# A relational graph layer with residual and normalisation: the low parts of x go from GpSimd to VectorE, the variance step the other way, and the order of three engines' programs is changed

## The chip, the core and the metric

One core of one Trainium2 chip. The kernel is one program on that core, with five instruction streams written out by hand: TensorE (PE), VectorE (DVE), ScalarE (ACT), GpSimd (POOL), and SyncE (SP), which only issues DMAs. They meet through semaphores. The metric is the device time of one execution in microseconds, median of several; lower is better.

## What is computed

The inputs are x (8 batches, 1024 rows, 128 features, fp32), adj (8 x 1024 x 1024, int32, mostly 0 and 1), four weights of 128 x 128 and a bias. Cut to what matters:

```python
rel_ids = arange(1, 5)
masks = (adj[None] == rel_ids[:, None, None, None])        # r b n m
h = einsum('rbnm,bmd->rbnd', masks, x)
y = einsum('rbnd,rdo->bno', h, weight) + bias
t = x + y
out = (t - mean(t)) / sqrt(var(t) + 1e-5)                   # over the 128 features
```

The fast path computes relation 1 alone, and on the way it finds out whether adj holds any value above 1. Only if it does, a second, general path behind a branch computes all again; with these inputs it is not entered.

## The kernel before, in words

**Tiling.** A batch of adj (4 MB) comes in 4 *units* of 1 MB, so there are 32 units, u = 0 to 31, two of them to a *half* (hf = 0 to 15), two halves to a batch (b = 0 to 7). Unit u is 2048 int32 to each of 128 partitions. Eight units fit in `adj_sb` (NADJ, L30), four batches of x (0.5 MB each) in `x_sb`.

**The way of a unit.** SP loads it. DVE converts it to bytes (`convert`, L425, the instruction is L429, tile `mask`, four buffers). PE *turns* it: four transposes into PSUM (`turn`, L558; L178, tile `tp_ps`, three buffers). ACT *expands* the turned bytes to fp32r (`expand`, L346; L350, tile `maskT`, four buffers). When both units of a half are expanded, PE multiplies them with x: 8 matmuls with the high part of x (`hi_products`, L577), 8 with the low part (`lo_products`, L586), all at L187. ACT copies the result to SBUF (`copy_half`, L353, L357), and PE projects it with the weight (`project_half`, L564: one matmul that spreads the bias, L194, and 8 at L199, tile `y_ps`, two buffers).

**The end of a half.** DVE adds x (`add_half`, L443, tile `total`), takes the statistics (`measure_half`: four at L205, four at L210), and adds epsilon to the variance (`lift_variance`, L214, tile `var_eps`). POOL (`scales`, L302) makes minus the mean (L307), the reciprocal root by a power (L217, tile `scale`), and their product (L312, tile `shift`). The four row tiles of the half are then normalised, two by DVE (`finish_half`, L221), one half later, and two by ACT (`finish_half`, L370), later still. SP stores whole batches once all loads are issued.

**The split of x.** For the products x is split into two fp32r parts. Before: DVE masks off bits to get `x_top` (`top`, L432, instruction L166, one buffer), POOL copies that to `x_hi` (`hi`, L293, L297), and POOL subtracts it from x to get `x_lo` (`lo`, L299, L170). Both parts have two buffers by batch. `x_top` of a batch waits until POOL has finished both parts of the batch before it.

**The order of the work.** Each engine executes its stream in order, and the order is that of the loops:

- SP (L239): unit 0, x of batch 0, then the units; x of batch 1 behind unit 3, of batch 2 behind unit 6, of batch b+1 behind unit 4b+2. A unit's load from u = 8 on waits for the conversion of unit u-8, x of batch b from b = 4 on for the last add of batch b-4.
- PE (L607): warm-up, the first half in quarters, and from hf = 2 (L628): hi products of hf, turn of unit 2hf+3, projection of half hf-1, lo products of hf, turn of unit 2hf+4.
- ACT (L387): copy of half hf-1, expansion of units 2hf+2 and 2hf+3, finish of half hf-3.
- DVE (L495 to L512): convert 0, top 0, the bias, converts 1 to 3, top 1, converts 4 and 5; then for hf = 1 to 14: converts 2hf+4 and 2hf+5, for even hf the top of batch hf/2+1, add and measure of half hf-1, finish of half hf-2.
- POOL (L318 to L331): split of the bias, hi and lo of batch 0, then for each b: hi of b+1, scales of half 2b-1, lo of b+1, scales of half 2b.

`place_bias` (L488) copies the three bf16 parts of the bias, each repeated four times, into `bias_parts`; its three copies (L491) stand ahead of convert 1.

## Time and profile before

| what | value |
|---|---|
| median of 3 runs | 118.46 us (117.81 to 120.78) |
| the profiled execution, its own time | 118.53 us |
| its span in the profile | 116.7 us |
| PE busy | 102.6 us (88%) |
| DVE busy | 95.0 us (81%) |
| ACT busy | 84.6 us (72%) |
| POOL busy | 75.7 us (65%) |
| DMA, mean over the span | 361 GB/s, about 420 GB/s until all is loaded |
| granted clock of TensorE, mean | 0.991 of full speed |

The span runs from the first to the last instruction that the profile records; 1.83 us of the execution's own time lie outside it. Busy shares are means over a head that fills the pipe, a long middle in which the same half is repeated, and a tail. Weight loads run beside matmuls and are listed as an engine of their own (PEld). The ends of matmuls are modelled, so a group of 8 that is shown as 2.1 us may be followed by the next group after 1.87 us.

### The profile page before, as it was taken

The numbers are of one execution on the slowest core, as the hardware profiler recorded it, in microseconds if no ns is written. First come the engines' busy times: TensorE is split into PE (matmuls) and PEld (weight loads), VectorE is DVE, ScalarE is ACT, GpSimd is POOL, SyncE is SP. The second block draws the span as 40 slices with busy tenths as digits, with TensorE's granted clock in tenths as the row PEclk, the third lists the DMA queues.
The fourth block names the chain that finished last, engine by engine and source line by source line (L and its number), as shares of the span: only waits on it lengthen the run. The fifth ranks groups of instructions, "written<-read, shape, count | busy, mean of one in ns | idle before, by whom it ended". The sixth has DMA issues, their size and how long they took to land.

```text
span 116.7 us, 1943 instructions
## 1 busy us (share of the span) xinstructions
PE 102.6 (88%) x587; PEld 85.5 (73%) x587; DVE 95.0 (81%) x242; ACT 84.6 (72%) x114; POOL 75.7 (65%) x78
## 2 busy tenths in 40 slices
PE   5966379994999999999999999999999999999800
PEld 2333378683889888888898889898888888889600
DVE  0089967633989899999999999999999999996960
ACT  0433199179868997899999999999999889974410
POOL 6069038000095998599759898999899759953640
PEclk9999999999999999999999999999999999999996
DMA  3999999999999999999999999999999997030441
GB/s 87 396 433 429 415 438 427 415 432 418 418 424 424 424 424 417 417 424 424 414 431 421 414 428 413 429 413 427 421 427 418 404 420 314 10 142 38 171 152 53
DMA packets 7362, 42.16 MB, mean 361 GB/s; under 512 B 819, under 2 KB 1206, under 8 KB 3254
## 3 DMA queue, kind: packets, MB, share of 16 engines
q1 hardware_dynamic: 7200, 41.95, 86.9%
q8 instruction: 6, 0.10, 0.4%
q10 hardware_dynamic: 150, 0.07, 0.2%
q14 instruction: 6, 0.05, 0.1%
HBM read 37.82 MB, written 4.19 MB: 360 GB/s over the span
## 4 chain that ended last, share of the span: by engine, by line
PE 48%; DMA 21%; DVE 15%; POOL 8%; issue 3%; ACTq 1%; POOLq 0%; DVEq 0%
PE h_ps L187 32%; DMA adj_sb<-in_adj_dram 17%; PE y_ps L199 8%; PE tp_ps L178 7%; DMA bias_rows<-in_L_gnn_bias_dram 4%; DVE bias_parts L491 4%; POOL scale L217 4%; DVE mask L429 3%; DVE stats L205 3%; POOL x_lo L170 2%; DVE total L443 2%; PE y_ps L194 2%; DVE var_eps L214 2%; DVE mean_var L210 1%; ACTq L379 1%
## 5 line engine op out<-in xcount | busy, mean ns | idle before, releaser
L350 ACT ACTIVATE maskT<-tp_ps 128x2048 fp32r<-128x2048 fp8e5 x32 | 60.2, 1881 | 14.9 <-PE tp_ps L178 14.8
L429 DVE TENSOR_SCALAR mask<-adj_sb 128x2048 uint8<-128x2048 uint32 x32 | 39.5, 1267 | 12.4 <-DMA adj_sb<-in_adj_dram 12.4
L217 POOL TENSOR_TENSOR scale<-var_eps,power 128x4 f32<-128x4 f32 (+1 forms) x17 | 36.3, 2137 | 0.9 <-DVE var_eps L214 0.7
L187 PE MATMUL h_ps<-maskT,x_hi 128*128 128x512 f32 (+1 forms) x144 | 34.2, 379 | 2.6 <-ACT maskT L350 2.5
L187 PE MATMUL h_ps<-maskT,x_lo 128*128 128x512 f32 (+1 forms) x144 | 34.3, 380 | 0.4 <-POOL x_lo L170 0.4
L187 PEld LDWEIGHTS h_ps<-maskT,x_hi 128*128 128x128 f32 x144 | 24.3, 189 | 7.7 <-ACT maskT L350 3.9
L187 PEld LDWEIGHTS h_ps<-maskT,x_lo 128*128 128x128 f32 x144 | 24.1, 189 | 4.5 <-POOL x_lo L170 0.7
L178 PEld LDWEIGHTS tp_ps<-identity,mask 128*128 128x128 f32 x128 | 19.8, 202 | 6.4 <-DVE mask L429 2.7
L178 PE MATMUL tp_ps<-identity,mask 128*128 128x128 f32 x128 | 20.2, 281 | 3.4 <-DVE mask L429 3.4
L170 POOL TENSOR_TENSOR x_lo<-x_sb,x_top 128x1024 fp32r<-128x1024 f32 x8 | 19.2, 2402 | 0.0
L307 POOL TENSOR_SCALAR minus_mean<-mean_var 128x4 f32<-128x4 f32 (+1 forms) x16 | 4.0, 248 | 22.5 <-DVE var_eps L214 21.6
L199 PEld LDWEIGHTS y_ps<-w_sb,h_sb 128*128 128x128 f32 x128 | 16.7, 192 | 1.2 <-ACT h_sb L364 0.7
L199 PE MATMUL y_ps<-w_sb,h_sb 128*128 128x128 f32 x128 | 17.2, 276 | 0.3 <-ACT h_sb L364 0.3
L205 DVE BATCH_NORM_STATS2 stats<-total 128x6 f32<-128x128 f32 x64 | 14.1, 281 | 1.3
L370 ACT ACTIVATE out_sb<-total,shift,scale 128x128 f32<-128x128 f32 x31 | 13.5, 484 | 0.8 <-POOL shift L312 0.6
L297 POOL CAST x_hi<-x_top 128x1024 fp32r<-128x1024 f32 x8 | 8.3, 1041 | 6.9 <-DVE x_top L166 6.9
L357 ACT ACTIVATE h_sb<-h_ps 128x512 f32<-128x512 f32 x14 | 8.4, 599 | 5.5 <-issue 5.5
L443 DVE TENSOR_TENSOR total<-y_ps,x_sb 128x512 f32<-128x512 f32 (+1 forms) x17 | 11.0, 650 | 0.8 <-PE y_ps L199 0.8
L221 DVE TENSOR_SCALAR out_sb<-total,mean_var,scale 128x128 f32<-128x128 f32 x33 | 9.9, 339 | 0.6 <-POOL scale L217 0.6
L214 DVE TENSOR_SCALAR var_eps<-mean_var 128x4 f32<-128x4 f32 (+1 forms) x17 | 8.3, 485 | 1.7
L605 PE MATMUL h_ps<-warm 128*128 128x512 bf16 x24 | 7.6, 478 | 1.4 <-POOL warm L275 1.4
L312 POOL TENSOR_TENSOR shift<-minus_mean,scale 128x4 f32<-128x4 f32 (+1 forms) x16 | 6.0, 372 | 2.1
(30 smaller groups left out, 40.4 us busy)
## 6 DMA issues: line engine op xcount, KB each, us to landing
adj_sb<-in_adj_dram SPq DMA_DIRECT2D x32, 1024.0 KB, 18.0
x_sb<-in_x_dram SPq DMA_DIRECT2D x8, 512.0 KB, 12.1
out_dram<-out_sb SPq DMA_DIRECT2D x7, 512.0 KB, 18.5
out_dram<-out_sb SPq DMA_DIRECT2D x1, 256.0 KB, 2.3
out_dram<-out_sb SPq DMA_DIRECT2D x2, 128.0 KB, 2.6
w_sb<-in_L_gnn_weight_dram ACTq DMA_DIRECT2D x1, 64.0 KB, 7.1
bias_rows<-in_L_gnn_bias_dram ACTq DMA_DIRECT2D x3, 0.5 KB
```

What stands on the lines that cost most here:

```text
L170: eng.tensor_tensor(flat(x_lo[:, slot]), flat(x_sb[:, x_slot]), flat(x_top[:, :]).bitcast(fp32), ALU.subtract).then_inc(done, 1)
L178: last = nc.tensor.transpose(tp_ps[:, bank, place:place + P], words[:, o, j], identity[:, :])
L187: last = nc.tensor.matmul(h_ps[:, bank, 0:n], (x_hi, x_lo)[part][:, slot, t, :], maskT[:, places, t // WORD, t % WORD, :], start=(first an ...
L199: last = nc.tensor.matmul(y[:, n, :], h_of(r)[:, s], w_sb[:, r, :], start=False, stop=(r == relations - 1 and s == tiles.stop - 1))
L205: last = nc.vector.bn_stats(stats[:, slot, s, :], total[:, place, s, :])
L214: nc.vector.tensor_scalar(var_eps[:, slot, tiles], mean_var[:, slot, tiles, 1], EPS, None, ALU.add).then_inc(done, by)
L217: nc.gpsimd.tensor_tensor(scale[:, slot, tiles], var_eps[:, slot, tiles], power[:, tiles], ALU.pow).then_inc(done, by)
L221: last = nc.vector.tensor_scalar(out_sb[:, b, s, :], total[:, place, s, :], mean_var[:, slot, s, 0:1], scale[:, slot, s:s + 1], ALU.subtra ...
L350: nc.scalar.activation(maskT[:, u % NMT], turned_codes(u % NTP), ACT.Copy, accum_out=counts[:, u:u + 1]).then_inc(expanded, 1)
L370: last = nc.scalar.activation(out_sb[:, b, s, :], total[:, b % NTOTAL, s, :], ACT.Identity, bias=shift[:, b % 2, s:s + 1], scale=scale[:, ...
L429: nc.vector.tensor_scalar(mask[:, u % NMASK], adj_sb[:, u % NADJ].bitcast(u32), CAP, SET, ALU.min, ALU.mult).then_inc(masked, 1)
L443: nc.vector.tensor_tensor(total[:, b % NTOTAL, tiles], y, x_sb[:, b % NX, tiles], ALU.add).then_inc(added, by)
```

## The change

`x_top` is gone. POOL makes `x_hi` by a copy of x that rounds to fp32r (DVE does it for batch 0), and DVE makes `x_lo`, as x minus `x_hi`, for all batches. The step that adds epsilon to the variance goes from DVE to POOL, as the first instruction of `scales`. DVE's stream is shifted by one conversion: in iteration hf it converts units 2hf+3 and 2hf+4 (was 2hf+4 and 2hf+5); at its start the bias copies stand behind convert 2 and are a quarter as wide. PE projects half hf-1 ahead of the turn of unit 2hf+3. ACT finishes half hf-3 between its two expansions. SP loads x of batch b+1 behind unit 4b+3. The bias matmul reads one row block of the bias, repeated by its access pattern. The diff without its declarations and without the general path (which gets the same split of x):

```diff
--- before.py
+++ after.py
@@ -68,7 +66,7 @@
         bias_rows = sb("bias_rows", [P, D], fp32)
         bias_rest = sb("bias_rest", [P, D], fp32)
         bias_fine = sb("bias_fine", [P, D], fp32)
-        bias_parts = sb("bias_parts", [P, HT, D], bf16)
+        bias_parts = sb("bias_parts", [P, D], bf16)
         spread = sb("spread", [P, P], bf16)
         identity = sb("identity", [P, P], fp32)
         ones = sb("ones", [P, P], fp32)
@@ -162,12 +159,8 @@
         def store(eng, b, place, tiles, done):
             eng.dma_start(out_p[b][:, tiles.start * D:tiles.stop * D], flat(out_sb[:, place, tiles])).then_inc(done, 16)
 
-        def take_top(x_slot, done):
-            nc.vector.tensor_scalar(flat(x_top[:, :]), flat(x_sb[:, x_slot]).bitcast(u32), TOP_BITS, None,
-                                    ALU.bitwise_and).then_inc(done, 1)
-
         def take_lo(eng, x_slot, slot, done):
-            eng.tensor_tensor(flat(x_lo[:, slot]), flat(x_sb[:, x_slot]), flat(x_top[:, :]).bitcast(fp32),
+            eng.tensor_tensor(flat(x_lo[:, slot]), flat(x_sb[:, x_slot]), flat(x_hi[:, slot]).bitcast(fp32),
                               ALU.subtract).then_inc(done, 1)
 
         def turn_words(of, bank, done):
@@ -191,7 +184,8 @@
 
         def spread_bias(y, tiles):
             n = tiles.stop - tiles.start
-            nc.tensor.matmul(y[:, 0:n, :], spread[:, :], bias_parts[:, 0:n, :], start=True, stop=False)
+            nc.tensor.matmul(y[:, 0:n, :], spread[:, :], bias_parts[:, :].unsqueeze(1).to_broadcast([P, n, D]),
+                             start=True, stop=False)
 
         def project(h_of, y, relations, tiles, done, by):
             for n, s in enumerate(range(tiles.start, tiles.stop)):
@@ -210,8 +204,8 @@
                 last = nc.vector.bn_aggr(mean_var[:, slot, s, :], stats[:, slot, s, :])
             last.then_inc(done, by)
 
-        def lift_variance(slot, tiles, done, by):
-            nc.vector.tensor_scalar(var_eps[:, slot, tiles], mean_var[:, slot, tiles, 1], EPS, None, ALU.add).then_inc(done, by)
+        def lift_variance(eng, slot, tiles, done, by):
+            eng.tensor_scalar(var_eps[:, slot, tiles], mean_var[:, slot, tiles, 1], EPS, None, ALU.add).then_inc(done, by)
 
         def row_scales(slot, tiles, done, by):
             nc.gpsimd.tensor_tensor(scale[:, slot, tiles], var_eps[:, slot, tiles], power[:, tiles], ALU.pow).then_inc(done, by)
@@ -240,7 +234,7 @@
             load_batch(0)
             for u in range(1, UNITS):
                 load_unit(u)
-                if u % CH == (2 if u >= CH else 3) and u // CH + 1 < B:
+                if u % CH == CH - 1 and u // CH + 1 < B:
                     load_batch(u // CH + 1)
             for b in range(LAST):
                 sp.wait_ge(normed, CH * (b + 1))
@@ -280,7 +274,7 @@
                                     channel_multiplier=1).then_inc(const_set, 1)
             nc.gpsimd.memset(power[:, :], -0.5).then_inc(const_set, 1)
             nc.gpsimd.memset(spread[:, :], 1.0).then_inc(const_set, 1)
-            nc.gpsimd.memset(bias_parts[:, :, :], 0.0).then_inc(bias_split, 1)
+            nc.gpsimd.memset(bias_parts[:, :], 0.0).then_inc(bias_split, 1)
 
             def split_bias():
                 pool.wait_ge(bias_loaded, 16 * len(PARTS))
@@ -291,21 +285,22 @@
                                         ALU.subtract).then_inc(bias_split, 1)
 
             def hi(b):
-                pool.wait_ge(topped, b + 1)
-                if b >= 2:
+                pool.wait_ge(x_loaded[b % NX], 16 * (b // NX + 1))
+                if b == 1:
+                    pool.wait_ge(lo_made, 1)
+                else:
                     pool.wait_ge(multiplied, CH * (b - 1))
-                nc.gpsimd.tensor_copy(flat(x_hi[:, b % 2]), flat(x_top[:, :]).bitcast(fp32)).then_inc(hi_made, 1)
-
-            def lo(b):
-                take_lo(nc.gpsimd, b % NX, b % 2, lo_made)
+                nc.gpsimd.tensor_copy(flat(x_hi[:, b % 2]), flat(x_sb[:, b % NX])).then_inc(hi_made, 1)
 
             def scales(b, tiles, count, by):
-                pool.wait_ge(var_ready, count)
+                pool.wait_ge(aggregated, count)
                 if b >= 2:
                     pool.wait_ge(normed, CH * (b - 1))
                     pool.wait_ge(act_normed, CH * (b - 1))
+                lift_variance(nc.gpsimd, b % 2, tiles, var_ready, by)
                 nc.gpsimd.tensor_scalar(minus_mean[:, b % 2, tiles], mean_var[:, b % 2, tiles, 0], -1.0, 0.0,
                                         ALU.mult, ALU.add).then_inc(negated, by)
+                pool.wait_ge(var_ready, count)
                 row_scales(b % 2, tiles, scaled, by)
                 pool.wait_ge(scaled, count)
                 pool.wait_ge(negated, count)
@@ -316,17 +311,15 @@
                 scales(hf // 2, HALF[hf % 2], 2 * (hf + 1), 2)
 
             split_bias()
-            hi(0)
-            lo(0)
             for b in range(B):
                 if b + 1 < B:
                     hi(b + 1)
                 if b >= 1:
                     scales_half(2 * b - 1)
-                if b + 1 < B:
-                    lo(b + 1)
                 scales_half(2 * b)
             scales(LAST, QUARTER[2], 2 * (HALVES - 1) + 1, 1)
+            pool.wait_ge(aggregated, 2 * HALVES)
+            lift_variance(nc.gpsimd, LAST % 2, QUARTER[3], var_ready, 1)
             pool.wait_ge(var_ready, 2 * HALVES)
             row_scales(LAST % 2, QUARTER[3], scaled, 1)
@@ -384,13 +376,14 @@
             expand(2)
             copy_quarter(0, 1)
             expand(3)
-            for hf in range(1, HALVES - 1):
-                if hf >= 2:
-                    copy_half(hf - 1)
+            expand(4)
+            expand(5)
+            for hf in range(2, HALVES - 1):
+                copy_half(hf - 1)
                 expand(2 * hf + 2)
-                expand(2 * hf + 3)
                 if hf >= 3:
                     finish_half(hf - 3)
+                expand(2 * hf + 3)
             copy_half(HALVES - 2)
             finish_half(HALVES - 4)
             copy_quarter(HALVES - 1, 0)
@@ -429,12 +422,9 @@
                 nc.vector.tensor_scalar(mask[:, u % NMASK], adj_sb[:, u % NADJ].bitcast(u32), CAP, SET,
                                         ALU.min, ALU.mult).then_inc(masked, 1)
 
-            def top(b):
-                dve.wait_ge(x_loaded[b % NX], 16 * (b // NX + 1))
-                if b >= 1:
-                    dve.wait_ge(hi_made, b)
-                    dve.wait_ge(lo_made, b)
-                take_top(b % NX, topped)
+            def lo(b):
+                dve.wait_ge(hi_made, b + 1)
+                take_lo(nc.vector, b % NX, b % 2, lo_made)
 
             def add(b, y, tiles, count, by):
                 dve.wait_ge(projected, count)
@@ -449,8 +439,6 @@
             def variances(b, tiles, count, by):
                 dve.wait_ge(measured, count)
                 aggregate_rows(b % 2, tiles, aggregated, by)
-                dve.wait_ge(aggregated, count)
-                lift_variance(b % 2, tiles, var_ready, by)
 
             def finish(b, tiles, count, by):
                 dve.wait_ge(scaled, count)
@@ -488,24 +476,25 @@
             def place_bias():
                 dve.wait_ge(bias_split, 3)
                 for q, part in zip(PARTS, (bias_rows, bias_rest, bias_fine)):
-                    last = nc.vector.tensor_copy(bias_parts[q:q + 1], upper(part[q:q + 1, :]).unsqueeze(1).to_broadcast(
-                        [1, HT, D]))
+                    last = nc.vector.tensor_copy(bias_parts[q:q + 1, :], upper(part[q:q + 1, :]))
                 last.then_inc(bias_split, 1)
 
             convert(0)
-            top(0)
+            dve.wait_ge(x_loaded[0], 16)
+            nc.vector.tensor_copy(flat(x_hi[:, 0]), flat(x_sb[:, 0])).then_inc(hi_made, 1)
+            lo(0)
+            convert(1)
+            convert(2)
             place_bias()
-            for u in (1, 2, 3):
-                convert(u)
-            top(1)
+            convert(3)
             convert(4)
-            convert(5)
+            lo(1)
             for hf in range(1, HALVES - 1):
-                for u in (2 * hf + 4, 2 * hf + 5):
+                for u in (2 * hf + 3, 2 * hf + 4):
                     if u < UNITS:
                         convert(u)
                 if hf % 2 == 0 and hf // 2 + 1 < B:
-                    top(hf // 2 + 1)
+                    lo(hf // 2 + 1)
                 add_half(hf - 1)
                 measure_half(hf - 1)
                 if hf >= 2:
@@ -627,9 +616,8 @@
             turn(6)
             for hf in range(2, HALVES - 1):
                 hi_products(hf)
-                if 2 * hf + 3 < UNITS:
-                    turn(2 * hf + 3)
                 project_half(hf - 1)
+                turn(2 * hf + 3)
                 lo_products(hf)
                 if 2 * hf + 4 < UNITS:
                     turn(2 * hf + 4)
```

## Rows read from the trace of the kernel before

**Rows 1.** The page's first line: span and instructions of the profiled execution.

```profile
span 116.7 us, 1943 instructions
```

**Rows 2.** Windows view, all engines: stretch and its length, then busy us (instructions), clock.

```profile
51.20:74.20 23.00, 23.00 (x133) 20.11 (x132) 22.02 (x60) 20.75 (x28) 19.76 (x17) 1.00 1.01 421
```

**Rows 3.** The chain that ended last: start us, us, engine, tile, line.

```profile
72.56 1.86 PE h_ps L187 x8
74.41 0.46 PE tp_ps L178 x4
...
77.20 0.22 PE y_ps L194
77.41 0.89 PE y_ps L199 x8
...
101.68 3.08 PE h_ps L187 x16
```

**Rows 4.** Timeline of the head: start us, us, engine, line, operation, tiles, count.

```profile
9.27 2.49 DVE L491 COPY bias_parts<-bias_rest 1x512 bf16<-1x512 bf16 x1
...
28.02 2.13 PE L187 MATMUL h_ps<-maskT,x_hi 128*128 128x512 f32 x8 [1.58 <-ACT maskT L350]
...
31.66 1.23 DVE L429 TENSOR_SCALAR mask<-adj_sb 128x2048 uint8<-128x2048 uint32 x1
```

**Rows 5.** DMA view, issues between 6.5 and 8 us: count, KB, us to landing.

```profile
adj_sb<-in_adj_dram SPq DMA_DIRECT2D x1, 1024.0 KB, 23.9
```

**Rows 6.** Timeline of VectorE (DVE) over one batch, 80.4 to 92.4 us.

```profile
80.42 0.68 DVE L166 TENSOR_SCALAR x_top<-x_sb 128x1024 uint32<-128x1024 uint32 x1
81.02 0.68 DVE L443 TENSOR_TENSOR total<-y_ps,x_sb 128x512 f32<-128x512 f32 x1
81.80 0.87 DVE L205 BATCH_NORM_STATS2 stats<-total 128x6 f32<-128x128 f32 x4
...
82.71 0.38 DVE L210 BATCH_NORM_AGGREGATE mean_var<-stats 128x2 f32<-128x6 f32 x4
...
83.19 0.17 DVE L214 TENSOR_SCALAR var_eps<-mean_var 128x4 f32<-128x4 f32 x1
83.27 0.60 DVE L221 TENSOR_SCALAR out_sb<-total,mean_var,scale 128x128 f32<-128x128 f32 x2
...
83.78 2.36 DVE L429 TENSOR_SCALAR mask<-adj_sb 128x2048 uint8<-128x2048 uint32 x2
...
86.05 0.68 DVE L443 TENSOR_TENSOR total<-y_ps,x_sb 128x512 f32<-128x512 f32 x1
...
88.23 1.45 DVE L214 TENSOR_SCALAR var_eps<-mean_var 128x4 f32<-128x4 f32 x1
...
92.38 0.68 DVE L166 TENSOR_SCALAR x_top<-x_sb 128x1024 uint32<-128x1024 uint32 x1
```

**Rows 7.** Timeline of GpSimd (POOL) over the same batch.

```profile
83.67 3.34 POOL L217 TENSOR_TENSOR scale<-var_eps,power 128x4 f32<-128x4 f32 x1
...
87.14 0.20 POOL L312 TENSOR_TENSOR shift<-minus_mean,scale 128x4 f32<-128x4 f32 x1
87.29 2.37 POOL L170 TENSOR_TENSOR x_lo<-x_sb,x_top 128x1024 fp32r<-128x1024 f32 x1
...
93.13 1.04 POOL L297 CAST x_hi<-x_top 128x1024 fp32r<-128x1024 f32 x1 [0.61 <-DVE x_top L166]
```

**Rows 8.** Line L217, 28 to 104 us: count, ns min/median/max, first and last start.

```profile
L217 POOL TENSOR_TENSOR scale<-var_eps,power x13: 1073/2530/3947, 32.9 to 102.0; 128x4 f32<-128x4 f32 x13
```

**Rows 9.** Groups by line and form, L443 at half width: busy us, mean ns.

```profile
L443 DVE TENSOR_TENSOR total<-y_ps,x_sb 128x256 f32<-128x256 f32 x2 | 0.8, 414 | 0.0
```

**Rows 10.** Timeline, 82 to 85 us: one turn on TensorE and its expansion on ScalarE.

```profile
82.34 0.63 PE L178 MATMUL tp_ps<-identity,mask 128*128 128x128 f32 x4
...
83.00 1.88 ACT L350 ACTIVATE maskT<-tp_ps 128x2048 fp32r<-128x2048 fp8e5 x1 [0.28 <-PE tp_ps L178]
...
84.77 0.20 ACT L350 ACTIVATION_READ_ACCUMULATOR maskT<-tp_ps 128x1 f32 x1
```

More of the change, by code:

```diff
@@ L10 @@
 FULL = 2048.5
-TOP_BITS = 0xFFFFF000
 def relational_layer(nc, x, adj, weight, bias, out):
@@ L62, in relational_layer @@
         x_sb = sb("x_sb", [P, NX, TILES, D], fp32)
-        x_top = sb("x_top", [P, TILES, D], u32)
         x_hi = sb("x_hi", [P, 2, TILES, D], fp32r)
@@ L107, in relational_layer @@
         expanded = sem("expanded")
-        topped = sem("topped")
         hi_made = sem("hi_made")
@@ L129, in relational_layer @@
         g_loaded = sem("g_loaded")
-        g_topped = sem("g_topped")
+        g_hi_made = sem("g_hi_made")
         g_split = sem("g_split")
@@ L336, in _ @@
                 with pool.Fori(0, B) as b:
-                    pool.wait_ge(g_topped, b + 1)
+                    pool.wait_ge(g_hi_made, b + 1)
                     take_lo(nc.gpsimd, 0, 0, g_split)
-                    nc.gpsimd.tensor_copy(flat(x_hi[:, 0]), flat(x_top[:, :]).bitcast(fp32)).then_inc(g_split, 1)
                     pool.wait_ge(g_var_ready, b + 1)
@@ L532, in _ @@
                     nc.vector.memset(scratch[:, 0:1], 0.0)
-                    take_top(0, g_topped)
+                    nc.vector.tensor_copy(flat(x_hi[:, 0]), flat(x_sb[:, 0])).then_inc(g_hi_made, 1)
                     for r in range(R):
@@ L550, in _ @@
                     dve.wait_ge(g_aggregated, b + 1)
-                    lift_variance(0, ALL, g_var_ready, 1)
+                    lift_variance(nc.vector, 0, ALL, g_var_ready, 1)
                     dve.wait_ge(g_scaled, b + 1)
@@ L660, in _ @@
                                 turn_words(mask[:, ch], ch % NTP, g_turned)
-                            pe.wait_ge(g_split, 2 * (b + 1))
+                            pe.wait_ge(g_split, b + 1)
                             pe.wait_ge(g_expanded, CH * R * b + CH * r + 2 * half + 2)
```

## The prediction, made before the changed kernel was run

> **What bounds the kernel now.** I read the page first (the span is 116.7 us [rows 1]; the profiled execution took 118.53 us, so 1.83 us lie outside, and it stands 0.07 us above the median of the runs), then the windows, the chain, and the timelines of the engines.
>
> In the middle TensorE is the bound: 23.00 us busy in a stretch of 23.00, at full granted clock, while VectorE is busy for 22.02, ScalarE 20.75 and GpSimd 19.76 [rows 2]. The reader is to see how close the others are: VectorE has 1 us in 23 to spare. One half costs TensorE, by the chain's steps, 1.86 for the hi products, 0.46 for a turn, 0.22 and 0.89 for bias and projection, as much again as the first two for the lo products and the second turn: 2 x 1.86 + 2 x 0.46 + 1.11 = 5.75 us, 11.5 a batch [rows 3]. This runs from the hi products of half 2 at 28.02 [rows 4] to the lo products of half 14 at 101.68 [rows 3]. Behind them come 116.7 - 101.7 = 15.0 us of tail.
>
> The loads matter in the head alone: unit 8 was issued once unit 0 was converted, at about 6.9 us, and took 23.9 to land [rows 5], so it is there at 30.8, just before its conversion at 31.66 [rows 4].
>
> **The head.** The bias copies stood ahead of convert 1; the second took 2.49 us and ended at 11.76 [rows 4]. Now converts 1 and 2 go first, behind x_hi and x_lo of batch 0 (about 0.7 and 1.2 us, sized below), beside the landing of unit 1. Products of halves 1 and 2 can come some 2 us earlier than 28.02. But hi of half 3 stands behind the turn of unit 8, and unit 8 doesn't land earlier: its conversion ends at 30.8 + 1.2 = 32.0 instead of 32.9 (31.66 + 1.23 [rows 4]). So 0.9 of the 2 us can outlive it. Then comes the new order: convert 9 is no longer next. It stands behind lo of batch 2, add, measure and finish.
>
> **VectorE over a batch.** In steps from start to start [rows 6]: top 0.60, add 0.78, statistics 0.91, aggregates 0.48, epsilon step 0.08, two normalisations 0.51, two conversions 2.27, and for the second half 2.18 from the add at 86.05 to the epsilon step at 88.23, which with what follows it takes until 92.38. In that last 4.15 there are 0.51 and 2.27 again and 1.37 for the epsilon step. Sum 11.96 us. The change removes the top (0.60), both epsilon steps (0.08 + 1.37) and the wait for the aggregates ahead of each (about 0.08 twice, since the aggregates end 0.10 before the step and 0.03 is usual): 11.96 - 2.2 = 9.75. It adds lo. The trace has no subtraction of 1024 elements from SBUF on VectorE. The add is 0.68 us for 512 [rows 6] and 0.414 for 256 [rows 9]; continued by the same slope that is 1.2 us for 1024. From below it is bounded by the top, 0.68 us for 1024 with one source [rows 6], from above by the same subtraction on GpSimd, 2.37 [rows 7]. I take 1.2, or 1.15 as a step. So 10.9 us of work a batch: less than TensorE's 11.5, if VectorE never waits.
>
> The Trainium skill (VectorE: DVE Perf Modes, Side-by-side) keeps a tensor_tensor of fp32 at one element a cycle, with about 150 cycles of start; by that page lo would be (1024 + 158) / 0.96 GHz = 1.23 us, an estimate that no row here can confirm.
>
> **The wait that the change adds.** It does wait. Lo of batch c+1 (in iteration hf = 2c) waits for x_hi of that batch, which GpSimd now makes behind scales of half 2c-2 in its own stream. VectorE aggregates that half in iteration 2c-1, and between this and lo stand only the normalisations and two conversions. Before, nothing that VectorE needed within the same iteration stood behind those scales. Count from the end A of the aggregates:
>
> - VectorE: normalisations 0.5, conversions until A + 2.9; it could start lo at A + 2.8.
> - GpSimd: it takes the epsilon step at about A + 0.15 (0.2 us, as minus the mean), and the power at A + 0.5, right with the first conversion. The power takes 1.07 at the least, 2.53 in the median and 3.95 at most [rows 8]. In rows 7 it starts at 83.67, 0.11 ahead of two conversions that end at 86.14 [rows 6], and ends at 87.01, so 0.87 behind them. In the median (2.53) it ends about 0.3 behind them, and its product is done 0.3 later. I take A + 2.9 + 0.6; bounds are A + 2.9 (product done with the conversions) and A + 2.9 + 1.2 (87.14 + 0.20 against 86.14).
> - The cast: 1.04 [rows 7], and 0.1 for the semaphore.
>
> Lo starts at A + 4.64, 1.84 late (bounds 1.2 and 2.45). VectorE then needs 10.9 + 1.84 = 12.74 us a batch (12.1 to 13.35), above TensorE's 11.5. It becomes the bound. Queued behind the waiting lo are add, statistics, and conversions 4c+5 and 4c+6: the turn of unit 4c+5 on TensorE waits for them, and what is behind it.
>
> **The sum.** Lo of batch 2 starts at 31.98 (GpSimd is in time there, since VectorE waits for unit 8 itself). Then lo 1.15, add 0.78, statistics 0.91, aggregates 0.41, normalisations 0.51, conversion 1.22: unit 9 is ready at 36.96. Five periods later, lo being waited for in iterations 4, 6, 8, 10 and 12, unit 29 is ready: 36.96 + 5 x 12.74 = 100.66. From there TensorE: turn 0.46, lo 1.86, turn 0.46, hi 1.86, projection 1.11, turn 0.46 [rows 3] and 0.05 for the start make 6.26: lo of half 14 starts at 106.92 instead of 101.68, 5.24 later. The tail holds the epsilon step of the last quarter on GpSimd instead of VectorE, one hop more: 0.15. Span 116.7 + 5.24 + 0.15 = 122.1, time 122.1 + 1.83 = 123.9 us, 4.6% more than the median.
>
> **What I cost at nothing.** GpSimd loses 2.37 us a batch and gains two epsilon steps of 0.2; it waits between scales anyway. The narrower bias copies and the repeated read of the bias: the copies now lie beside the landing of unit 3, the matmul writes the same columns. If that cover is gone, under 0.5 us once. SP: unit 4b+3 is issued ahead of x of the next batch instead of behind it and no longer waits for its add, so it lands 1.2 us earlier and x 2.5 us later; x is needed by the cast a full half later. Loads are issued eight units ahead, so a slower VectorE finds them landed. ACT's finish needs a product made over an iteration before. The projection ahead of the turn moves the turn of unit 2hf+3 by 1.11: from its start to the end of its expansion are 84.97 - 82.34 = 2.63 us [rows 10], and with lo and the second turn TensorE gives it 0.46 + 1.86 + 0.46 = 2.78. That is hidden by 0.15 us, and if it isn't, it costs up to 0.1 a half where TensorE is the bound, nothing where VectorE is.
>
> **Rivals.**
>
> - *The cast gets in between (119.9 us).* If power and product are done early (1.07 at the least [rows 8]) the cast can start before the conversions end. It then holds one of them, as x_lo held the epsilon step: 88.23 + 1.45 ends with x_lo at 89.66 [rows 6, 7]. VectorE loses 1.04 instead of 1.84, a period of 11.94: 5 x 0.8 = 4.0 us less than forecast. Against it: the power starts no earlier against the conversions than before, and only its shortest durations allow it. The Trainium skill (GPSIMD Engine Reference, Specifications) says that GpSimd shares its SBUF interfaces with VectorE, with contention when VectorE uses two ports or reads two SBUF inputs. The page doesn't say who wins; rows 7 show the power losing to conversions, rows 6 the epsilon step losing to x_lo.
> - *The wait costs nothing (117.8 us, not slower).* If x_hi is made by A + 3.4, the period stays under 11.5, and TensorE is the bound from the turn of unit 9 at 37.0. Then hi of half 4 is at 37.0 + 2.78 = 39.8, ten halves of 5.75 give 97.3 for half 14, its lo comes 1.86 + 1.11 + 0.46 later, at 100.7, 1.0 before the present one: 116.7 - 1.0 + 0.15 + 1.83 = 117.7 to 117.8. The point: a wait of at most 0.6 us. For it: the work itself fits (10.9). Against: the cast alone takes 1.04, behind a product that ends with the conversions at the earliest.
> - *The head's gain is kept whole (115.5 us).* As the last, and with units 8 and 9 ready when TensorE wants them: some 2.3 us less. Against it the landing of unit 8 at 30.8.
> - *The worst of both (over 127.5 us).* Period 13.35 and a lo of 2.37: 123.9 + 5 x (0.6 + 1.2) = 132.9; with the period alone 127.
>
> **Chances.** Forecast (period 12.1 to 13.35) 0.62, its own range 120.7 to 127; cast in between 0.14; no cost 0.13; head kept 0.07; worst 0.04. The range takes in the cheap wait and the long power: 119.0 to 127.5. A measurement tells about 2% from no change here. Slower by more (over 120.8): the forecast, the worst, and a part of the second case, 0.69. Faster (below 116.1): 0.06, from the fourth case. Within: 0.25.
>
> **What would show it.** Waits of VectorE for x_hi at the subtraction, six of them, the later ones near 1.8 us; TensorE waiting for conversions at the turns of units 9, 13, 17 to 29, about 1.2 us each; its busy share in the middle near 90%; the cast starting right behind the product of an even half; lo near 1.2 us; the tail from the lo products of half 14 about 15.1 us. It is wrong if the casts end before the conversions do, or if TensorE is gapless in the middle.

## The result, and the profile after

The changed kernel took 127.29 us in the median of four runs (126.94 to 128.82), beside 118.72 for the kernel before: a ratio of 1.072, with an interval of 1.064 to 1.081. It is slower by 7%. A kernel's executions fall into a faster and a slower group, and here and below a median is over all of them, a ratio and its interval over the faster group alone. I had forecast 123.9, with 119.0 to 127.5 as the range: direction and mechanism hold, the amount was 3.4 us short. The profiled execution is the longest of the four, 128.82 us.

The page's first line, the granted clock of slice after slice, and two groups of the changed kernel:

```profile
span 127.1 us, 1928 instructions
...
PEclk9999999968999999999999999999999995999997
...
L208 POOL TENSOR_SCALAR var_eps<-mean_var 128x4 f32<-128x4 f32 (+1 forms) x17 | 30.5, 1793 | 42.0 <-DVE mean_var L204 35.2
...
L163 DVE TENSOR_TENSOR x_lo<-x_sb,x_hi 128x1024 fp32r<-128x1024 f32 x8 | 9.9, 1232 | 13.0 <-POOL x_hi L293 13.0
```

The second group is the wait that the prediction put there: VectorE stands idle for 13.0 us ahead of the subtractions. The first is one that it had not seen: adding epsilon to four numbers takes 1.79 us in the mean on GpSimd, where the kernel before had 0.17 and 1.45 for it on VectorE [rows 6].

The waits of the changed kernel, in all, times, longest:

```profile
DVE x_lo L163 <- POOL x_hi L293: 13.0, 5, 2.7
...
PE tp_ps L171 <- DVE mask L422: 12.0, 9, 2.3
```

The middle by windows, to be read beside [rows 2]: 26 us of the changed kernel.

```profile
50.00:76.00 26.00, 23.68 (x132) 19.67 (x132) 20.41 (x55) 20.51 (x28) 17.35 (x19) 1.00 1.01 422
```

TensorE, which had no gap before, now has 2.3 us of gaps in 26; VectorE, ScalarE and GpSimd have more room than they had. No engine is full. What sets the pace is a loop through two of them, and the timeline of GpSimd and VectorE over one turn of that loop shows it. It answers to [rows 6] and [rows 7]:

```profile
79.87 0.38 DVE L204 BATCH_NORM_AGGREGATE mean_var<-stats 128x2 f32<-128x6 f32 x4
80.17 0.57 DVE L215 TENSOR_SCALAR out_sb<-total,mean_var,scale 128x128 f32<-128x128 f32 x2
80.40 2.65 POOL L208 TENSOR_SCALAR var_eps<-mean_var 128x4 f32<-128x4 f32 x1 [0.51 <-DVE mean_var L204]
80.66 2.35 DVE L422 TENSOR_SCALAR mask<-adj_sb 128x2048 uint8<-128x2048 uint32 x2
83.13 0.19 POOL L301 TENSOR_SCALAR minus_mean<-mean_var 128x4 f32<-128x4 f32 x1
83.28 1.04 POOL L211 TENSOR_TENSOR scale<-var_eps,power 128x4 f32<-128x4 f32 x1
84.45 0.20 POOL L307 TENSOR_TENSOR shift<-minus_mean,scale 128x4 f32<-128x4 f32 x1
84.59 1.04 POOL L293 CAST x_hi<-x_sb 128x1024 fp32r<-128x1024 f32 x1
85.66 1.23 DVE L163 TENSOR_TENSOR x_lo<-x_sb,x_hi 128x1024 fp32r<-128x1024 f32 x1 [2.65 <-POOL x_hi L293]
86.80 0.68 DVE L433 TENSOR_TENSOR total<-y_ps,x_sb 128x512 f32<-128x512 f32 x1
```

The reader is to see the order. The aggregates end at 80.25. The epsilon step starts at 80.40, 0.26 ahead of the two conversions, and doesn't end until they do, at 83.0. Power and product come wholly behind that, then the cast, and then, at 85.66, the subtraction, for which VectorE has waited 2.65 us. The cast starts as the product ends, so it waits for its place in GpSimd's stream and not for a free buffer of x_hi. Add, statistics, the next two conversions and so TensorE's next turn stand behind it. In this trace the subtractions of batches 2 and 7 start at 32.64 and 99.39: 13.35 us a batch, where TensorE's own work is 11.5.

One of the five waits of this trace is 2.39 us. There the epsilon step gets through in 0.23, and the next small step, minus the mean, is held instead:

```profile
67.29 0.23 POOL L208 TENSOR_SCALAR var_eps<-mean_var 128x4 f32<-128x4 f32 x1 [0.50 <-DVE mean_var L204]
67.54 2.36 DVE L422 TENSOR_SCALAR mask<-adj_sb 128x2048 uint8<-128x2048 uint32 x2
67.59 2.36 POOL L301 TENSOR_SCALAR minus_mean<-mean_var 128x4 f32<-128x4 f32 x1
72.29 1.23 DVE L163 TENSOR_TENSOR x_lo<-x_sb,x_hi 128x1024 fp32r<-128x1024 f32 x1 [2.39 <-POOL x_hi L293]
```

Either way power and product stand wholly behind the conversions. The epsilon step was 0.25 ahead of them here, as it was where it was held.

### The profile page after: what moved, and what is told of

Its sections match the earlier page's. It is cut to its first block, busy times and chain, and to the rows that moved or that the text cites. A ratio compares the mean times of both kernels' runs of the same rounds, so it can differ in the third digit from the quotient of the medians.

```text
span 127.1 us, 1928 instructions
## 1 busy us (share of the span) xinstructions
PE 106.9 (84%) x586; PEld 86.1 (68%) x587; DVE 87.7 (69%) x226; ACT 83.9 (66%) x114; POOL 66.0 (52%) x86
## 4 chain that ended last, share of the span: by engine, by line
PE 41%; DMA 23%; DVE 20%; POOL 8%; issue 4%; POOLq 1%; ACT 0%; DVEq 0%
PE h_ps L180 26%; DMA adj_sb<-in_adj_dram 23%; DVE mask L422 9%; PE tp_ps L171 7%; PE y_ps L193 6%; POOL var_eps L208 4%; DVE stats L199 4%; DVE total L433 3%; DVE out_sb L215 2%; POOL scale L211 2%; PE y_ps L187 2%; POOL x_hi L293 2%; DVE mean_var L204 1%; DVE x_lo L163 1%; POOLq L327 0%
## 5 line engine op out<-in xcount | busy, mean ns | idle before, releaser
L208 POOL TENSOR_SCALAR var_eps<-mean_var 128x4 f32<-128x4 f32 (+1 forms) x17 | 30.5, 1793 | 42.0 <-DVE mean_var L204 35.2
L180 PE MATMUL h_ps<-maskT,x_hi 128*128 128x512 f32 (+1 forms) x144 | 35.5, 390 | 0.4 <-ACT maskT L342 0.3
L180 PE MATMUL h_ps<-maskT,x_lo 128*128 128x512 f32 (+1 forms) x144 | 35.7, 392 | 0.0
L171 PE MATMUL tp_ps<-identity,mask 128*128 128x128 f32 x128 | 21.9, 295 | 12.0 <-DVE mask L422 12.0
L180 PEld LDWEIGHTS h_ps<-maskT,x_lo 128*128 128x128 f32 x144 | 25.4, 198 | 4.0
L163 DVE TENSOR_TENSOR x_lo<-x_sb,x_hi 128x1024 fp32r<-128x1024 f32 x8 | 9.9, 1232 | 13.0 <-POOL x_hi L293 13.0
L211 POOL TENSOR_TENSOR scale<-var_eps,power 128x4 f32<-128x4 f32 (+1 forms) x17 | 17.0, 999 | 0.1
L293 POOL CAST x_hi<-x_sb 128x1024 fp32r<-128x1024 f32 x7 | 7.3, 1038 | 6.5 <-DMA x_sb<-in_x_dram 6.5
L204 DVE BATCH_NORM_AGGREGATE mean_var<-stats 128x2 f32<-128x6 f32 x64 | 6.2, 158 | 0.6
L187 PE MATMUL y_ps<-bias_parts,spread 128*128 128x512 bf16 (+1 forms) x17 | 6.4, 377 | 0.0
## 6 DMA issues: line engine op xcount, KB each, us to landing
x_sb<-in_x_dram SPq DMA_DIRECT2D x8, 512.0 KB, 13.1
```

What stands on the lines that cost most here:

```text
L163: eng.tensor_tensor(flat(x_lo[:, slot]), flat(x_sb[:, x_slot]), flat(x_hi[:, slot]).bitcast(fp32), ALU.subtract).then_inc(done, 1)
L171: last = nc.tensor.transpose(tp_ps[:, bank, place:place + P], words[:, o, j], identity[:, :])
L180: last = nc.tensor.matmul(h_ps[:, bank, 0:n], (x_hi, x_lo)[part][:, slot, t, :], maskT[:, places, t // WORD, t % WORD, :], start=(first an ...
L208: eng.tensor_scalar(var_eps[:, slot, tiles], mean_var[:, slot, tiles, 1], EPS, None, ALU.add).then_inc(done, by)
L211: nc.gpsimd.tensor_tensor(scale[:, slot, tiles], var_eps[:, slot, tiles], power[:, tiles], ALU.pow).then_inc(done, by)
```

## The experiments

Each is the changed kernel with one edit, if not said otherwise. Times are medians, and the ratio is to the kernel before on the same chip, whose median was 120.9 for 1 to 8, 119.5 for 9 to 11 and 119.4 for 12.

**1. The subtraction behind the finish.** VectorE's work is the same, in another order.

```diff
                 for u in (2 * hf + 3, 2 * hf + 4):
                     if u < UNITS:
                         convert(u)
-                if hf % 2 == 0 and hf // 2 + 1 < B:
-                    lo(hf // 2 + 1)
                 add_half(hf - 1)
                 measure_half(hf - 1)
                 if hf >= 2:
                     finish_half(hf - 2)
+                if hf % 2 == 0 and hf // 2 + 1 < B:
+                    lo(hf // 2 + 1)
```

> The changed kernel with one move on VectorE: the subtraction that makes x_lo of batch c+1 stands behind the finish of its iteration instead of ahead of the add. Its work is the same. Theory A (the wait for x_hi behind the scales on GpSimd sets the period): by then x_hi is nearly there (aggregates, normalisations, two conversions, add, statistics, aggregates, normalisations come to 5.4 us, the cast ends near 5.6), VectorE waits 0.3 us at most, the period falls from 13.3 to TensorE's 11.5, the time to 118 to 119 us. Theory B (VectorE's own work, or the conversions that come one later, sets the period): VectorE does the same work in the same number of instructions, the period stays above 12.5 and the time above 124 us.

118.25 us, ratio 0.979 (0.960 to 0.998). Theory A holds, B falls: the same work in the same conversions' order, and all of the loss is gone. No wait for x_hi is left in its trace.

**2. The cast ahead of the scales.** VectorE's order is untouched; GpSimd's is changed, and x_hi gets a third buffer (with the waits that its reuse needs; these lines are left out here and in 10 to 12).

```diff
             for b in range(B):
-                if b + 1 < B:
-                    hi(b + 1)
+                if b == 0:
+                    hi(1)
                 if b >= 1:
                     scales_half(2 * b - 1)
+                if b + 2 < B:
+                    hi(b + 2)
                 scales_half(2 * b)
```

> The changed kernel with VectorE's order as it is, and one move on GpSimd: the cast to x_hi of batch c+1 stands ahead of the scales of half 2c-2 instead of behind them, which takes a third buffer for x_hi. Theory A: VectorE's wait at the subtraction, 2.65 us each time, is gone (under 0.3), the period is TensorE's 11.5, the time 117.5 to 119 us. Theory B: as the work and the order of VectorE are unchanged, the period stays above 12.5 and the time above 124. If the wait is gone and the time lies between 120 and 124, conversions coming late at the turn (the second half of theory B) have a part of their own.

117.25 us, ratio 0.978 (0.965 to 0.990). The order of the queue on GpSimd made the loss. The third buffer is part of this edit, but experiment 1 removes the loss without it, and in the changed kernel the cast never waited for a buffer. With the cast moved in it, VectorE waits nowhere for x_hi, though its stream still asks for it at the same place. In the second half of the middle TensorE is gapless again:

```profile
64.00:96.00 32.00, 32.00 (x186) 26.95 (x185) 29.96 (x74) 28.09 (x40) 24.90 (x25) 1.00 1.01 419
```

**3. The epsilon step back on VectorE.**

```diff
                 aggregate_rows(b % 2, tiles, aggregated, by)
+                dve.wait_ge(aggregated, count)
+                lift_variance(nc.vector, b % 2, tiles, var_ready, by)
...
-                pool.wait_ge(aggregated, count)
+                pool.wait_ge(var_ready, count)
...
-                lift_variance(nc.gpsimd, b % 2, tiles, var_ready, by)
```

> The changed kernel with the epsilon step back on VectorE, so that GpSimd starts again with minus the mean. It tells what moving the epsilon step costs. In the trace of the changed kernel that step is held on GpSimd for 2.65 us by the two conversions and the power (1.04) and the product run wholly behind them. Theory A with this as the mis-sized term: the power starts ahead of the conversions again, the product ends 0.6 us behind them instead of 1.6, the wait falls to about 1.65 us while VectorE gains 0.35 us of work a batch: a period of 12.65 instead of 13.3, time lower by 5 x 0.65 = 3.3 us, about 124. Rival (the cast and the queue alone matter, whatever stands first in the scales): the wait stays at 2.6, the period rises to 13.6, time up by 1.5 us.

127.67 us, ratio 1.061 (1.044 to 1.077): as the changed kernel. Both expectations miss in part. Its timeline over the same place in the loop:

```profile
67.70 0.17 DVE L208 TENSOR_SCALAR var_eps<-mean_var 128x4 f32<-128x4 f32 x1
...
68.17 3.34 POOL L211 TENSOR_TENSOR scale<-var_eps,power 128x4 f32<-128x4 f32 x1
68.29 2.35 DVE L418 TENSOR_SCALAR mask<-adj_sb 128x2048 uint8<-128x2048 uint32 x2
71.64 0.20 POOL L305 TENSOR_TENSOR shift<-minus_mean,scale 128x4 f32<-128x4 f32 x1
71.78 1.04 POOL L293 CAST x_hi<-x_sb 128x1024 fp32r<-128x1024 f32 x1
72.85 1.22 DVE L163 TENSOR_TENSOR x_lo<-x_sb,x_hi 128x1024 fp32r<-128x1024 f32 x1 [2.21 <-POOL x_hi L293]
```

The wait falls from 2.65 to 2.21, not to 1.65. The power starts 0.12 ahead of the conversions and still ends 0.87 behind them, in the 3.34 form. What the wait gives back, VectorE spends again: the subtractions of batches 4 and 5 are 59.34 and 72.85, a period of 13.5. So where the epsilon step runs makes no difference to the time in this order that these few executions, on another chip than the first ones of the changed kernel, could show.

**4 and 8. Zeros multiplied while TensorE waits.** Matmuls of zeros into the PSUM bank that the turn then overwrites: 8 ahead of unit 6, 6 each ahead of units 13, 17, 21, 25 and 29. It ran twice, the second time beside the changed kernel itself (5).

```diff
-            def turn(u):
+            def turn(u, idle=0):
+                if idle:
+                    pe.wait_ge(expanded, u - NTP + 1)
+                    for _ in range(idle):
+                        nc.tensor.matmul(tp_ps[:, u % NTP], warm[:, 0:P], warm[:, :], start=True, stop=True)
                 pe.wait_ge(masked, u + 1)
...
-            turn(6)
+            turn(6, 8)
...
-                turn(2 * hf + 3)
+                turn(2 * hf + 3, 6 if hf % 2 == 1 and hf > 3 else 0)
```

> The changed kernel with matmuls on zeros while TensorE waits for a conversion: 8 ahead of the turn of unit 6, 6 ahead of the turns of units 13, 17 to 29; their results are overwritten. It tells what the clock costs. In the trace of the changed kernel the granted clock is at half from 26 to 29 us and from 104 to 107 us, in both places behind a gap of about 2 us, and 8 products take 3.4 and 3.6 us instead of 2.1. Theory C (the clock adds to the end): the clock stays at 1.00, and the time falls by the 1.5 us of the later place, 0.5 to 2 us in all, since the earlier one is partly hidden behind the landing of unit 8. Rival (the clock costs nothing that VectorE's period doesn't cover): no change within 0.3 us. The period of 13.3 stays in both.

> The same kernel as the one with zeros multiplied in the waits, now beside the changed kernel on one chip. Its trace showed the clock at 1.00 all through and 8 products of half 13 in 2.12 us. Theory C: faster than the changed kernel by 0.5 to 2 us. Rival: within 0.3 us of it, since most executions of the changed kernel do not have the second place.

> The changed kernel once more, unaltered, as the measure for the runs beside it: about 127 us, 1.06 to 1.07 of the kernel before; half clock near 27 us in its trace, with or without a second place near 105 us (theory C: with it the span is 1.5 us longer than without).

Once 127.06 us, once 125.99, the second with a ratio of 1.057 (1.051 to 1.064); the changed kernel beside it 127.69 (125.89 to 128.94). Two stretches by windows, of the changed kernel first (the last three columns are the granted clock, the share of DMA, and GB/s):

```profile
26.00:29.00 3.00, 3.00 (x10) 2.52 (x11) 2.89 (x10) 2.06 (x3) 0.98 (x1) 0.53 1.03 434
104.00:108.00 4.00, 3.72 (x12) 3.04 (x13) 3.86 (x14) 1.97 (x2) 3.29 (x5) 0.59 0.00 0
```

and of the kernel with the zeros:

```profile
26.00:29.00 3.00, 3.00 (x19) 2.44 (x19) 2.61 (x10) 2.09 (x3) 1.17 (x2) 1.00 1.03 431
104.00:108.00 4.00, 3.96 (x21) 3.44 (x22) 3.86 (x13) 3.18 (x4) 3.29 (x5) 1.00 0.00 0
```

The granted clock fell to the lower of its two levels (1.2 GHz) behind gaps of 2.3 and 1.9 us on TensorE, and with the zeros it doesn't in either trace. In the trace shown the later place costs 3.60 - 2.12 = 1.5 us, and it is on the path to the end:

```profile
104.28 0.90 PE L171 MATMUL tp_ps<-identity,mask 128*128 128x128 f32 x4 [1.89 <-DVE mask L422]
104.84 3.60 PE L180 MATMUL h_ps<-maskT,x_lo 128*128 128x512 f32 x8
```

Not every execution has it. The other trace of the changed kernel (5, span 124.8) has the same products, behind a gap of 1.86 us, at full clock:

```profile
103.98 2.10 PE L180 MATMUL h_ps<-maskT,x_lo 128*128 128x512 f32 x8
```

So the clock explains part of the scatter of the changed kernel. That the zeros make the kernel faster is not shown. The changed kernel beside them took 125.9 and 126.5, and twice 128.9 at a mean granted clock of 0.955 and 0.956; the five executions with the zeros took 125.2 to 127.0, none with a clock under 0.984. The whole 1.7 us between the medians rests on those two executions, and the first set has nothing (127.06, where the changed kernel had 127.29 on another chip). The waits and the period are as before in both.

**6. A second cast, unused.** Ahead of the real one for batches 3 to 7.

```diff
...
+                if b >= 3:
+                    nc.gpsimd.tensor_copy(flat(spare[:, :]), flat(x_sb[:, b % NX])).then_inc(spared, 1)
+                    pool.wait_ge(spared, b - 2)
                 nc.gpsimd.tensor_copy(flat(x_hi[:, b % 2]), flat(x_sb[:, b % NX])).then_inc(hi_made, 1)
```

> The changed kernel with a second, unused cast of the same size ahead of the cast to x_hi of batches 3 to 7 on GpSimd (1.04 us and 0.1 for a semaphore). Theory A: every bit of it goes into VectorE's wait, 3.7 us instead of 2.65 five times, the period rises from 13.3 to 14.4 and the time by 5 x 1.1 = 5.6 us. Theory B (VectorE's own work and order set the period): GpSimd has the room for it, no change within 1 us.

133.23 us, ratio 1.117 (1.108 to 1.126): 5.5 us more than the changed kernel beside it by the medians. The trace is of its longest execution, 135.36 us. Each of the five waits is 3.77 us, 1.12 more than 2.65. The subtractions come every 14.52 us, beside 13.35 and 13.21 in the two traces of the changed kernel, which makes 5.9 to 6.6 us over five batches. GpSimd is busy for 53% of the span, and yet 1.1 us more of it at this place costs 1.2 to 1.3 us a batch:

```profile
102.86 1.04 POOL L296 CAST spare<-x_sb 128x1024 fp32r<-128x1024 f32 x1
103.96 1.05 POOL L298 CAST x_hi<-x_sb 128x1024 fp32r<-128x1024 f32 x1
...
105.05 1.23 DVE L165 TENSOR_TENSOR x_lo<-x_sb,x_hi 128x1024 fp32r<-128x1024 f32 x1 [3.77 <-POOL x_hi L298]
```

(Lines of two timelines of that kernel, GpSimd's and VectorE's.)

**7. The conversions in the old order.**

```diff
             lo(1)
+            convert(5)
             for hf in range(1, HALVES - 1):
-                for u in (2 * hf + 3, 2 * hf + 4):
+                for u in (2 * hf + 4, 2 * hf + 5):
```

> The changed kernel with VectorE's conversions back in the order of before (units 2hf+4 and 2hf+5 in iteration hf); the wait for x_hi is as it was. Theory A: the loop of VectorE and GpSimd is the same, period 13.3 and waits 2.65; but TensorE now waits for unit 2hf+4 at the end of its iteration instead of for 2hf+3 in the middle, so the same lateness is felt a turn and 8 products (2.3 us) later: the time falls by about 2.3 us once, to 124.5 to 125.5. Theory B (the order of the conversions sets the period): the period falls below 12.5 and the time below 122.

126.53 us, ratio 1.065 (1.052 to 1.077). That is 1.2 less than the median of the changed kernel beside it, but two of that kernel's four executions took 125.9 and 126.5, and the spans of the two traces are 124.3 and 124.8. So no gain is shown, where I had expected 2.3 us. Period and waits are unchanged (the subtractions come every 13.1 us), so theory B falls here too. In the trace the 2.3 us are there but paid for beforehand: now units 8 and 9 are both converted ahead of the first subtraction of the loop, and unit 9 lands later, so the loop starts at 35.01 instead of 32.52.

**9 to 11. What is left of the rest.** 9 is the kernel before with the bias copies as in the change; 10 is the version of experiment 2 with the old order of conversions and turn; 11 is that version again.

```diff
...
             convert(0)
             top(0)
-            place_bias()
-            for u in (1, 2, 3):
-                convert(u)
+            convert(1)
+            convert(2)
+            place_bias()
+            convert(3)
             top(1)
```

> The kernel before with one part of the change alone: the copies of the bias a quarter as wide and behind convert 2. Everything else is as before, so top, cast and lo of GpSimd, the epsilon step on VectorE, conversions and projection in the old order. I expect the products of half 2 about 2 us earlier, of which the landing of unit 8 leaves 0.5 to 1: 0.4 to 0.9% faster than before, 117.5 to 118.2 us if before is 118.5. If it is over 1.5% faster, the head alone is what the version with x_hi ahead of the scales gains; if it is the same as before, the gain of that version has another source.

> The version with the cast ahead of the scales (third buffer of x_hi), and both reorderings taken back: conversions 2hf+4 and 2hf+5, the turn of unit 2hf+3 ahead of the projection. Left of the change are the split of x, the epsilon step, the bias and the head. In the trace of the version with them TensorE has no gap from half 9 on and a half costs 5.79 us, 0.03 more than before. I expect 116.3 to 117.3, up to 1 us faster than that version: 0.4 from the turn (12 x 0.03), and 0.5 from conversion 9 being early in the head. If it is slower, the reorderings were worth something with the wait gone.

> The version with the cast ahead of the scales once more, beside the two others on one chip: 1.5 to 3% faster than the kernel before.

118.12, 117.44 and 117.48 us, ratios 0.993 (0.988 to 0.997), 0.990 (0.985 to 0.995) and 0.992 (0.987 to 0.997). Experiments 2 and 11 are the same kernel: 0.978 in the first set, 0.992 in this one with more executions, where I had expected 1.5 to 3%. With the wait out of the way the whole change is worth about 1%, as much as the head alone within the measurement. The two reorderings are worth nothing either way: I had expected up to 1 us from taking them back.

**12. The best version with a warm head.** Experiment 2 with 6 matmuls of zeros ahead of unit 6 and 2 ahead of unit 8.

```diff
...
-            turn(6)
+            turn(6, 6)
...
-                    turn(2 * hf + 4)
+                    turn(2 * hf + 4, 2 if hf == 2 else 0)
```

> The version with the cast ahead of the scales (third buffer of x_hi), with matmuls on zeros in the two waits of the head: 6 ahead of the turn of unit 6, 2 ahead of that of unit 8. In the second trace of that version the granted clock is at 0.50 from 26 to 28 us, behind a gap of 2.1 us, and the hi products of half 2 take 3.4 us. Theory C: the clock stays at 1.00 there, half 3 starts up to 1.2 us earlier, the time falls by 0.3 to 1 us, to 116.3 to 117.2, or 1 to 2% under the kernel before. Rival: the landing of unit 8 covers it, the time stays at 117.4 within 0.2 us.

117.34 us, ratio 0.987 (0.981 to 0.993). The clock stays up, and nothing comes of it: the rival holds. The trace shows what covers it:

```profile
32.49 2.11 PE L181 MATMUL h_ps<-maskT,x_hi 128*128 128x512 f32 x8
...
36.47 0.74 PE L171 MATMUL tp_ps<-identity,mask 128*128 128x128 f32 x4 [0.76 <-DVE mask L425]
...
39.31 2.11 PE L181 MATMUL h_ps<-maskT,x_hi 128*128 128x512 f32 x8
```

Half 3 starts at 32.49 instead of 33.49 in experiment 11, but the turn of unit 9 then waits for its conversion, and half 4 starts at 39.31 in the one and 39.36 in the other. The kernel before had 39.58 there. Nor is the clock down there every time without the zeros: in the trace of experiment 2, the same kernel as 11, the gap ahead of unit 6 is 0.96 us, the hi products of half 2 take 2.13, and half 4 starts at 39.23.

## Why the prediction was right in kind and short in amount

**The hit.** The median of 127.29 us lies in the range of 119.0 to 127.5 by 0.2 us, above the forecast's own 120.7 to 127, and the repeat's 127.69 (5) is outside both. That the range held is in part luck.

**What bounds the kernel, and the work of VectorE.** Right. The subtraction takes 1.23 us (taken: 1.2). With no wait VectorE fits under TensorE, as experiments 1 and 2 show.

**The head.** Right in its waits, 0.5 to 0.7 us short in its sum. Unit 8 was there at about 30.7 and bounded the subtraction of batch 2, and the conversion of unit 9 came late. Half 3 starts at 33.82, as before: the hi products of half 2 ran at half clock, 3.44 us, and TensorE came to the turn of unit 8 after it had been converted. With the zeros (4) half 3 starts at 33.01. The claim that GpSimd is in time for batch 2 missed something: the cast for it ran from 30.60, and the conversion of unit 8, begun at 30.73, took 1.98 us instead of 1.23. In the versions without the wait (1, 2, 9 to 12) half 4 starts between 39.23 and 39.69, beside 39.58 before: at most 0.35 us of the head's gain reaches it.

```profile
30.60 1.04 POOL L293 CAST x_hi<-x_sb 128x1024 fp32r<-128x1024 f32 x1
30.73 1.98 DVE L422 TENSOR_SCALAR mask<-adj_sb 128x2048 uint8<-128x2048 uint32 x1 [1.77 <-DMA adj_sb<-in_adj_dram]
```

**The wait that the change adds.** Its place, its cause, and what queues behind it are as predicted; experiments 1 and 2 remove it from either side, and 6 lengthens it one for one. Its size is the term that was off: 1.84 us forecast, 2.4 to 2.65 measured. Two parts. I took the median of the power, 2.53 us, from a mixture of forms [rows 8], for a product 0.6 us behind the conversions; with the epsilon step on VectorE it is the 3.34 form, the one shown in [rows 7], and the wait is 2.21 (experiment 3). That is 0.37. The rest, 0.18 to 0.44, is that the epsilon step, or minus the mean behind it, is held in the power's stead and leaves power and product wholly behind the conversions. I had given it 0.2 us, by the row of minus the mean, which stood behind a step of VectorE and ahead of the conversions. The sum also has a slip: a power of 2.53 us from A + 0.5 ends at A + 3.03, 0.13 behind the conversions and not 0.3, so by its own terms the wait was nearer 1.7.

**The wait appears five times, not six.** The sum had five; the list of what would show it said six. Batch 2's is covered by the wait for unit 8.

**The sum.** In the trace without the slow products (5) the subtraction of batch 2 starts at 32.52 against 31.98, that of batch 7 at 98.59: 66.07 / 5 = 13.21 against 12.74. The waits of that trace are 2.44 in the mean, 0.60 more than forecast, and the work between them 10.77 instead of 10.9. 0.54 + 5 x 0.47 = 2.9 us; the lo products of half 14 start at 109.76 against 106.92, 2.8 later. So these two terms are all of the error in that execution, of 126.49 us. In the other trace there are 1.5 us of half clock more, which the prediction had no term for.

**The tail.** 127.1 - 112.13 = 15.0 us, 15.15 forecast.

**The rivals.** *The cast gets in between* (119.9): no. The cast never came before the end of the conversions in the loop; in the head it did, and there it held one, as that rival had it. The Trainium skill (GPSIMD Engine Reference, Specifications) has the two engines share their SBUF interfaces. The traces agree in both directions: a conversion took 1.98 us beside a cast, an epsilon step 2.65 beside conversions. Who wins is not told by who starts first in the trace: the cast that started 0.13 ahead of its conversion kept its 1.04, the epsilon step that started 0.26 ahead of its two did not keep its 0.23. The traces agree with the page's second case too, VectorE reading two SBUF inputs. In experiment 1 the subtraction and two conversions follow each other, and minus the mean on GpSimd, begun 0.20 behind the start of the subtraction, lasts until the last of them ends (4 numbers to a partition, 3.34 us):

```profile
56.92 1.22 DVE L163 TENSOR_TENSOR x_lo<-x_sb,x_hi 128x1024 fp32r<-128x1024 f32 x1
57.12 3.34 POOL L301 TENSOR_SCALAR minus_mean<-mean_var 128x4 f32<-128x4 f32 x1
58.05 2.35 DVE L422 TENSOR_SCALAR mask<-adj_sb 128x2048 uint8<-128x2048 uint32 x2
```

*The wait costs nothing* (117.8): this is what experiments 1, 2 and 11 measure once the wait is taken away, 117.3 to 118.3. *The head's gain is kept whole*: no; unit 8 and the conversion of unit 9 hold it in every version.

## What to carry to other kernels

When a step moves to another engine, write down what stands ahead of it in that engine's stream and follow it back: an engine that is idle for nearly half of the time can still set the period, if it is asked for something behind a job that was given to it late. To test such a loop, move one instruction in one stream (here a move in either of the two streams worked) before touching the work. And where a small instruction contends with long ones, take the form of its duration that its place in the order gives, not the median over all its places.

## What the runs showed of the hardware that I had not expected

A GpSimd instruction of a few numbers can be held by conversions that begin after it, and need not be: in the two traces of the changed kernel the epsilon step started 0.24 to 0.26 us ahead of a pair of conversions 22 times, took 2.63 to 2.65 us in 16 of them, 0.23 in five and 1.51 in one. Where it took 0.23, minus the mean behind it took 2.35. The granted clock of TensorE can halve behind a single gap of about 2 us, and need not: the same place was at half clock behind a gap of 1.89 us in one trace and at full clock behind 1.86 in another. In the three traces with matmuls of zeros in the gap it stayed up.
